# Cross-attention with channel attention: the turned token probabilities are copied by ScalarE, sums come from a 41st value column, and the stacked values are sent batch by batch

## What is computed

```python
enc, ca = ctx[:, :124], ctx[:, 124:]
hs = mha(x @ Wq, enc @ Wk, enc @ Wv)              # token attention, 124 keys
ca_q1 = einsum('btc,th->bch', ca, Wq_ca)[:, indices]   # 128 of 192 channels
ca_hs1 = mha(ca_q1, x, x)                         # channel attention, 128 keys
ca_hs2 = mha(ca_hs1 @ Wq, ca @ Wk_ca, ca @ Wv_ca) # third attention, 4 keys
out = (hs + ca_hs2) @ Wout + b_out + x
```

## Time and profile before

| | |
|---|---|
| median of the runs | 269.14 us (267.83 to 273.08) |
| profiled execution, its own time | 267.8 us |
| its span in the trace | 265.7 us |
| TensorE busy | 231.2 us (87%) |
| weight loads busy | 214.4 us (81%) |
| VectorE busy | 200.1 us (75%) |
| ScalarE busy | 113.5 us (43%) |
| GpSimd busy | 52.9 us (20%) |
| mean granted TensorE clock | 0.968 of full speed |

### The profile page before, as it was taken

The page is one execution under the profiler, slowest core; times in us unless marked ns, Lnnn a source line. Parts: engine busy times, 40 slices in busy tenths (PEclk is TensorE's granted clock), DMA queues, the critical chain, the costliest instruction groups (busy, mean ns, idle before and its releaser), DMA issues.

```text
span 265.7 us, 5654 instructions
## 1 busy us (share of the span) xinstructions
PE 231.2 (87%) x1756; PEld 214.4 (81%) x1770; DVE 200.1 (75%) x547; ACT 113.5 (43%) x406; POOL 52.9 (20%) x135
## 2 busy tenths in 40 slices
PE   0289879999759997999799979997999799989984
PEld 0279767889648996899789978997899789987983
DVE  2764958779825897769897889788878887887683
ACT  3234634152405173337434733463445345424451
POOL 3230080033200332012500350035003500300000
PEclk9999977999968997999999999999999999999999
DMA  7992022027921410052005100520043002000101
GB/s 226 259 271 102 12 63 83 2 56 162 195 41 48 154 56 0 27 173 62 0 25 172 56 0 11 182 60 0 0 142 110 0 0 99 0 0 2 49 0 49
DMA packets 12180, 19.59 MB, mean 74 GB/s; under 512 B 1462, under 2 KB 8470, under 8 KB 12166
## 3 DMA queue, kind: packets, MB, share of 16 engines
q1 hardware_dynamic: 11343, 18.30, 24.8%
q10 hardware_dynamic: 823, 1.11, 1.5%
HBM read 14.17 MB, written 2.62 MB: 63 GB/s over the span
## 4 chain that ended last, share of the span: by engine, by line
PE 59%; DVE 23%; issue 6%; DMA 4%; SPq 4%; ACT 1%; DVEq 1%; ACTq 0%; POOL 0%
PE scores L1197 11%; PE bank_d L1222 10%; PE bank_d L1278 7%; PE bank_d L1049 6%; PE bank_a L1049 5%; DVE k_blocks L773 5%; SPq L396 4%; DVE neg_max L793 3%; PE turned L1044 3%; PE bank_d L1093 2%; DMA wca_t<-in_Wq_ca 2%; PE turned L1185 2%; DVE ca_less L681 2%; PE bank_d L1225 2%; DMA vw_stack<-vw_part 2%
## 5 line engine op out<-in xcount | busy, mean ns | idle before, releaser
L611 ACT ACTIVATE probs<-scores,neg_max 128x124 f32<-128x124 f32 x128 | 44.6, 377 | 12.3 <-DVE neg_max L793 12.3
L793 DVE TENSOR_REDUCE neg_max<-scores 128x4 f32<-128x512 f32 (+1 forms) x64 | 41.3, 676 | 4.0 <-PE scores L1169 1.9
L1049 PE MATMUL bank_a<-xT_r,wq_r 128*120 128x256 f32 (+1 forms) x192 | 29.1, 305 | 11.4 <-DVE xT_r L708 11.4
L600 ACT ACTIVATE probsT<-turned 128x512 f32<-128x512 f32 x32 | 17.4, 594 | 42.4 <-PE turned L1185 24.2
L1049 PEld LDWEIGHTS bank_a<-xT_r,wq_r 128*120 128x120 f32 (+1 forms) x192 | 25.8, 196 | 11.5 <-issue 11.4
L1222 PEld LDWEIGHTS bank_d<-xg,probsT 128*128 128x128 f32 x256 | 30.3, 193 | 2.8 <-issue 2.7
L1222 PE MATMUL bank_d<-xg,probsT 128*128 128x33 f32 x256 | 30.1, 272 | 2.5 <-ACT probsT L600 2.5
L1225 PE MATMUL bank_d<-v_sb,probsT 124*128 124x40 f32 x256 | 31.3, 278 | 0.0
L1225 PEld LDWEIGHTS bank_d<-v_sb,probsT 124*128 124x128 f32 x256 | 30.7, 192 | 0.0
L611 ACT ACTIVATION_READ_ACCUMULATOR probs<-scores,neg_max 128x1 f32 x128 | 28.1, 220 | 0.0
L1197 PE MATMUL scores<-k_blocks,qT 120*128 120x372 f32 (+2 forms) x96 | 24.6, 394 | 0.5 <-issue 0.2
(11 more groups left out here) (128 smaller groups left out, 401.8 us busy)
## 6 DMA issues: line engine op xcount, KB each, us to landing
xT<-in_x_cols SPq DMA_DIRECT2D x8, 384.0 KB, 3.8
x_h<-in_x_heads SPq DMA_DIRECT2D x8, 360.0 KB, 3.6
x_sb<-in_x SPq DMA_DIRECT2D x8, 320.0 KB, 3.3
vw_stack<-vw_part SPq DMA_DIRECT2D x16, 160.0 KB, 4.5
out<-out_sb SPq DMA_DIRECT2D x16, 160.0 KB, 1.8
ctxT<-in_ctx_cols SPq DMA_DIRECT2D x8, 256.0 KB, 4.0
wqT<-in_WqT ACTq DMA_DIRECT2D x1, 506.2 KB, 7.4
wq<-in_Wq ACTq DMA_DIRECT2D x1, 480.0 KB, 4.6
```

The source lines that it names most:

```text
L600: nc.scalar.activation(probsT[:, 4 * half:4 * half + 4, :], turned[half].rearrange("k (h q) -> k h q", h=4), ACT.Exp) \
L611: last = nc.scalar.activation(probs[:, h, 0:keys], scores[half][:, k * keys:(k + 1) * keys], ACT.Exp, bias=neg_max[:, h:h + 1], accum_out= ...
L793: v.tensor_reduce(neg_max[:, 4 * half:4 * half + 4], scores[half][:, 0:4 * keys].rearrange("q (h k) -> q h k", h=4), AX.X, ALU.max, negate ...
L1049: ins = mm(dst, stationary(w, half, c), moving(w, half, c), start=first and i == 0, stop=last and i == len(steps) - 1)
```

## The change

Four things are changed.

1. The copies of the turned token probabilities go from VectorE's list to ScalarE's.
2. The exponentials of the token units no longer accumulate sums. The value tile `v_sb` gets a 41st column of ones for each head, set once by GpSimd, the weighing matmuls are 41 columns wide, and `norm` takes its reciprocal from column 40 of the result in PSUM.
3. TensorE makes the next pair's channel scores before it turns the probabilities of unit 3. They now also wait for unit 3's exponentials.
4. The sixteen DMAs of the stacked values go out by quarters r, with all four slots of one quarter together, and count two semaphores. Pair 1 waits for the first eight alone. SyncE issues them ahead of its body of pair 0, not behind it.

In the diff the new `turned_copy` belongs to ScalarE, whose body calls it after `front(at, "QM")` for unit 2 and after `front(at, "QT01")` for unit 3; the removed calls are VectorE's.

```diff
-            body(At(0, 0, 0, "first"))
             sp.wait_ge(d_drained, RING_D.no(At(0, 0, 0, "first"), "VW3")[0] + 1)
-            for slot, part in enumerate(VW_PART):
-                for r in range(4):
+            for r in range(4):
+                for slot, part in enumerate(VW_PART):
                     sp.dma_start(
...
-                        vw_parts[part][HT * r:HT * r + HT].bitcast(F32)).then_inc(vw_stacked, 16)
+                        vw_parts[part][HT * r:HT * r + HT].bitcast(F32)).then_inc(vw_stacked[r // 2], 16)
+            body(At(0, 0, 0, "first"))
...
+            gp.memset(v_sb[:, :, :, :, D:D + 1], 1.0).then_inc(made, 1)
...
-                copy(v_sb[0:KEYS, par, b, :], src[0:KEYS, 0:HID]).then_inc(a_drained, 1)
+                copy(v_sb[0:KEYS, par, b, :, 0:D],
+                     src[0:KEYS, 0:HID].rearrange("k (h d) -> k h d", h=HEADS)).then_inc(a_drained, 1)
...
-                            bias=neg_max[:, h:h + 1], accum_out=sums[:, par, h:h + 1])
+                            bias=neg_max[:, h:h + 1])
...
+            def turned_copy(n, keys):
+                for half in range(2):
+                    act.wait_ge(turned_full, n * 2 + (half + 1))
+                    copy(probsT[0:keys, 4 * half:4 * half + 4, :],
+                         turned[half][0:keys, :].rearrange("k (h q) -> k h q", h=4)) \
+                        .then_inc(turned_out, 1)
...
-                dve.wait_ge(exped, n * 2 + 2)
-                v.reciprocal(recip[:, k % 2, :], sums[:, k % 2, :]).then_inc(inverted, 1)
-                src = piece(at, f"PV{k}")
+                src = piece(at, f"PV{k}")[:, 0:HEADS * (D + 1)].rearrange("q (h n) -> q h n", h=HEADS)
+                v.reciprocal(recip[:, k % 2, :], src[:, :, D]).then_inc(inverted, 1)
...
-                turned_copy(unit(at, 2), KEYS)   # VectorE's body
                 maxima(unit(at, 3), KEYS)
...
                 norm(at, 2)
-                turned_copy(unit(at, 3), KEYS)
...
                 weigh(at, 2)
+                if more:
+                    got_d(at, "MsT")
+
+                    pe.wait_ge(exped, unit(at, 3) * 2 + 2)
+                    channel_scores(unit(at, 4), at.next(), 0)
                 turn_probs(unit(at, 3), KEYS)
                 if more:
-                    got_d(at, "MsT")
-                    channel_scores(unit(at, 4), at.next(), 0)
...
-                pe.wait_ge(vw_stacked, 16 * 16)
+                pe.wait_ge(vw_stacked[0], 16 * 8)
+                if at == "epilogue" or at.b > 1:
+                    pe.wait_ge(vw_stacked[1], 16 * 8)
```

More of the change, by code:

```diff
@@ L196, in attention @@
         k_last = sb("k_last", [KL, 2, 2, 2, KEYS])
-        v_sb = sb("v_sb", [S, 2, 2, HID])
+        v_sb = sb("v_sb", [S, 2, 2, HEADS, D + 1])
         m = sb("m", [S, 2 * HT])
@@ L206, in attention @@
         probs = sb("probs", [S, HEADS, S])
-        sums = sb("sums", [S, 2, HEADS])
         recip = sb("recip", [S, 2, HEADS])
@@ L284, in attention @@
         vw_high = sem("vw_high")
-        vw_stacked = sem("vw_stacked")
+        vw_stacked = [sem("vw_stacked0"), sem("vw_stacked1")]
         def g_out(masked, src, r):
@@ L602, in exps_turned, with exps @@
                         .then_inc(exped, 1)
-            def exps(n, par, keys):
+            def exps(n, keys):
                 for half in range(2):
@@ L655, in body @@
                 exps_turned(unit(at, 1))
-                exps(unit(at, 2), 0, KEYS)
+                exps(unit(at, 2), KEYS)
                 if more:
                     front(at, "QM")
+                turned_copy(unit(at, 2), KEYS)
+                if more:
                     front(at, "MT")
@@ L661, in body @@
                     exps3(at)
-                exps(unit(at, 3), 1, KEYS)
+                exps(unit(at, 3), KEYS)
                 if not more:
@@ L666, in body @@
                     front(at, "QT01")
+                turned_copy(unit(at, 3), KEYS)
             pairs(act, body)
@@ L822, in place @@
                 last.then_inc(placed, 1)
[L824 to L829, removed]
             def norm(at, k):
@@ L843, in norm @@
                     return
-                dve.wait_ge(exped, n * 2 + 2)
-                v.reciprocal(recip[:, k % 2, :], sums[:, k % 2, :]).then_inc(inverted, 1)
-                src = piece(at, f"PV{k}")
+                src = piece(at, f"PV{k}")[:, 0:HEADS * (D + 1)].rearrange("q (h n) -> q h n", h=HEADS)
+                v.reciprocal(recip[:, k % 2, :], src[:, :, D]).then_inc(inverted, 1)
                 dve.wait_ge(inverted, n + 1)
                 v.tensor_tensor(hs[:, k - 2, 0:HID].rearrange("q (h d) -> q h d", h=HEADS),
-                                src[:, 0:HID].rearrange("q (h d) -> q h d", h=HEADS),
+                                src[:, :, 0:D],
                                 recip[:, k % 2, :].unsqueeze(2).broadcast_to([S, HEADS, D]),
@@ L1224, in weigh @@
                     else:
-                        last = mm(dst[:, h * D:(h + 1) * D], probsT[0:keys, h, :],
-                                  v_sb[0:keys, at.par, b, h * D:(h + 1) * D], start=True, stop=True)
+                        last = mm(dst[:, h * (D + 1):(h + 1) * (D + 1)], probsT[0:keys, h, :],
+                                  v_sb[0:keys, at.par, b, h, :], start=True, stop=True)
                     if k == 3 and h == HEADS - 2 and at.kind != "last":
@@ L1324, in body @@
                 if first:
-                    pe.wait_ge(made, 7)
+                    pe.wait_ge(made, 8)
                 weigh(at, 0)
```

## The result

The changed kernel takes 278.76 us, the median of four runs (278.0 to 279.73), against 268.49 us for the kernel before in the same session. The ratio is 1.040, with a 95% interval of 1.035 to 1.045: slower by 4%. The profiled execution took 278.0 us, of which the trace spans 276.2; before it was 267.8 and 265.7. I had forecast 272.0, between 265.5 and 276.5. Every ratio in this text leaves out executions that are over 1.5% above the fastest of their kernel (here the 273.08 us among the four of the kernel before), while the medians take in all of them.

What follows compares the result with a forecast made beforehand. TensorE was taken to bound the loop, busy 25.58 of 27.16 us a pass. 267.8 + 5.8 (late load) - 2.5 (seams) + 0.1 + 0.3 = 271.5, plus 0.5 for the median: 272.0 us, range 265.5 to 276.5.

Steps and rivals of the forecast that it cites:

- the seams' -2.5 us: At five seams between pairs, parts 1 and 3 remove a TensorE wait, saving 2.5 us in all; bounds 0 and -2.5.
- The first wait: TensorE's 0.49 us idle at a seam ahead of turning the split maxima; predicted to go, leaving passes of about 26.65 us.
- The late load: In pair 1, xT issued behind the sixteen stacked-value DMAs makes the first output 5.7 us later; carried as +5.8.
- I take the same: Half clock behind TensorE's idle time in pair 1: penalty kept at 2.4 us, bounds -1 to +1.5.
- The exchange of waits: In pair 1, TensorE's 3.86 us wait on the stacked values becomes one of some nine us on xT.
- The moved collision: Rival, chance 0.17: at the seams GpSimd's xT passes hold VectorE's split steps 0.5 us each; 275.5 us in all.
- 0.2 as a sign: At the seams, the last step of VectorE's split of the maxima would take 0.2 us in the profile after.
- the 0.9 us of lead: At the seams, VectorE's chain to the split maxima runs 0.9 us earlier, against a TensorE wait of 0.49.
- The 41st column: In the weighing matmuls, one more column costs 0.01 us, sixteen times: +0.1 us.
- The late reciprocal: At the kernel's end, the last hs starts 0.25 to 0.3 us later, all on the path: +0.3 us.
- The copies on ScalarE: At the seams, the moved probability copies hide in a ScalarE wait and behind the next pair's values, 0.7 us of cover.
- the loads come in time: Rival, chance 0.07: xT's landing does not hold pair 1, so its 3.86 us wait and 2.4 us half clock go; 259.4 us.

Runs made afterwards that it cites:

- e8: e1 with sixteen matmuls of no use in each body but the first, ahead of the turned channel scores: 256.88 us, ratio 0.960.
- e9: The changed kernel with sixteen matmuls of no use added in the seams: 268.75 us, ratio 1.006.
- e2: The kernel before with all of part 4 alone (quarters, two counts, issued ahead of SyncE's body of pair 0): 276.09 us, ratio 1.033.
- e4: The kernel before with the quarters and two counts, but the loads of pair 2 still ahead of the sixteen DMAs: 261.33 us, ratio 0.972.
- e5: e1 without part 3, so TensorE turns unit 3's probabilities before the channel scores: 284.23 us, ratio 1.059.
- e10: e5 with sixteen matmuls of no use added in the seams: 265.00 us, ratio 0.993.
- e12: e6 with the rounding of Wout, and GpSimd's difference of it, moved later in the prologue: 254.35 us, ratio 0.950.
- e1: The changed kernel with the loads of pair 2 again ahead of the sixteen stacked-value DMAs: 266.71 us, ratio 0.988.
- e6: e1 with the turns of hidden values and third-attention probabilities moved ahead of the turned channel scores: 255.01 us, ratio 0.954.
- e7: e4 with the turns of hidden values and third-attention probabilities moved ahead of the turned channel scores: 267.13 us, no ratio.
- e3: The changed kernel without any of part 4 (slot by slot, one count, behind SyncE's body of pair 0): 269.89 us, ratio 1.008.

## Why the prediction was wrong

The change of waits was foreseen and the time was not. By stretches, the profiled executions differ by 10.5 us: 1.4 ahead of pair 1, 6.7 in pair 1, 0.7 in pairs 2 to 6, and 1.7 from the start of pair 7 on. My sum for the same stretches was 0, +5.3, -2.0 and +0.4. In the profile of the second measurement the differences are -0.1, +5.9, +7.0 and +0.2.

- **The step that failed: the seams' -2.5 us, in which the clock has no price.** The first wait went as I said: a clean pass is 26.6 us, where I had 26.65. But pairs 2 to 6, where I had -2.0 (four seams; the fifth lies in pair 1), came to +0.7 us in the first profile and +7.0 in the second. In the first, three of the five passes begin at half clock, at 1.4 us each; in the second, the clock falls in three as well, two of them at 4.7 us. e8 and e9 show that this needs the idle time of the seam: with the wait filled by work for nothing, every one of these passes takes 26.5 us, and the changed kernel with its late load (e9) takes 268.75 us, under my 272.0. The kernel before had one such pass in its profile (28.39 us from 102.70), which the prediction does not mention. It was the sign that the seam could do it.
- **The late load: right in mechanism, short by 1.4 us in the first profile.** I said 5.8 us, of which 0.5 of seam gain in the same pass would come off, so 5.3; the pass is 6.7 longer. The issues took 12.74 us and not 11.71, which is +1.0. The landing took 4.50 where I had 5.1, and ScalarE's five steps 2.5 where I had 2.9, together -1.0. So the weighing began 10.95 us into the pass, where I had 10.8. From there to the first output I had 2.24 us, and the plain pass takes 1.99 (140.03 to 142.02). The rest is the next point.
- **"I take the same": a term too small.** I carried the half clock of pair 1 over at its old price, 2.4 us. Before, from the first output to the seam, pair 1 took 26.41 us (76.29 to 102.70) and a plain pass 23.96 (to 158.25), by this row of TensorE's timeline:

```profile
134.29 0.39 PE L1265 MATMUL bank_d<-vw_stack,probs3T 128*128 x1
```

That is 2.45 us of half clock. In the changed kernel, from the weighing to the seam, pair 1 took 29.50 us (81.33 to 110.83) and a plain pass 25.40 (140.03 to 165.43), which is 4.1 us: 1.65 more, and my upper bound was +1.5. The half clock held 5.1 us behind 3.86 idle ones, and about 10 us (80.08 to 90.20) behind 8.53 idle ones.

- **The exchange of waits: right.** SyncE's list, ScalarE's wait of 12.5 us (I said over 10), TensorE's of 9.1, though in two pieces (8.53 and 0.57): as described. e2 and e4 show it from both sides.
- **The moved collision: right in place, not in the order tested.** I gave it 0.17. In the changed kernel it caught L825 alone (0.67 us, where I had named 0.2 as a sign), which ended 0.5 us early enough. With the channel scores back behind the turns (e5, e10) it catches all four steps and holds TensorE for 1.0 us. So part 3, which I had priced as a part of the 0.9 us of lead, is what keeps part 1 from losing. "SBUF — State Buffer" of the Trainium skill, "Who interferes with whom", says that a VectorE instruction with two inputs in SBUF contends with a GpSimd instruction that reads SBUF, that copies and casts in a two-port mode contend with GpSimd too, and that the one that issues second is then fully blocked. The trace agrees: 0.55 to 0.64 us against 0.17 to 0.20, beside GpSimd passes of 0.70 us each.
- **The small terms.** The 41st column: a weighing takes 1.93 us in both kernels, so the difference is nothing, where I had +0.1. The late reciprocal: from the start of pair 7 to the last output's addition it is 23.95 us against 23.73, +0.2, and I had +0.3. The copies on ScalarE were hidden, as I said.
- **Of the execution and not of the kernel:** 1.5 us more from the last output's addition to the end of the span (3.7 against 2.2), and the 1.4 us ahead of pair 1. The second profile of the changed kernel has neither (2.3 us at the end, pair 1 from 68.85). The 3.7 us are there in the profiles of e2, e4 and e12 too, and not in the others. What makes them is open.

My rival "the loads come in time" gave 259.4; e1, where they do, has 266.7 in the median and 261.9 at its best, and e8, which is e1 with the clock kept up, 256.9. So that sum too lacked the price of the clock in the seams.

## What to carry to other kernels

In this kernel SyncE's queue was part of the critical path. When an issue block moves past others in one queue, list who waits for each of those, and count the issue time of the whole block (12.7 us here) and not only the landing. Price every idle stretch of TensorE twice, once as time and once as clock: a wait of one us in each pass cost 1.4 to 4.7 us where the clock fell. So try to put needed work into a wait that cannot be removed, even if it stood harmlessly behind it, and look at the clock of several executions: the loads put first took the ratio from 1.040 to 0.988 (e1), and the two moved turns took it to 0.954 (e6). On e4 the same move gained nothing that could be told (e7).

## What the runs showed of the hardware

- The granted clock fell from 2.4 to 1.2 GHz in seams where TensorE had idled 1.0 to 1.2 us, and not in others with the same gap: 110.83 against 138.82 in the changed kernel. Passes with more idle time but another length (e4: 27.17 us, waits of 0.49 and 1.04) kept full clock in every pass of the loop, while e7 had lost it behind waits of 0.49 and 0.64 us (96.84). What decides between them is not settled by these runs; that the fall stays away when the gap is filled is shown by e8 and e9.
- Sixteen matmuls of no use per pass made e1 9.8 us faster in the medians, and the changed kernel 10 (8 to 9 by the ratios), of which 2.8 us lie ahead of the first of them in the profiles.
- The sixteen DMAs took longer to issue quarter by quarter: 12.44 to 12.80 us in the twelve profiles with that order, against 11.71 and 11.15 us slot by slot (the kernel before and e3). Their number and sizes are the same; the quarters also count two semaphores in place of one, and no run parts the two. SyncE's rows of e3 and e2:

```profile
59.09 11.15 SPq L395 DMA_DIRECT2D vw_stack<-vw_part  x16
```

```profile
61.13 12.80 SPq L395 DMA_DIRECT2D vw_stack<-vw_part  x16
```
